# A two-layer decoder on one core: the four hand-written step orders of TensorE, VectorE, ScalarE and GpSimd rewritten

## The reference, cut to what matters

```
x = x + L0_attn(ln(x))           # m : state-space mixer: projections, a causal convolution with 16 decays, gate
x = x + L0_xattn(ln(x), ctx)     # x0: 16 heads of 8 against the context
x = x + L0_ffn(ln(x))            # s0: 16 heads of 4 over the 256 tokens, then 8 experts, the best two of each token
x = x + L1_attn(ln(x))           # s1: 16 heads of 8, 4 key heads, over the 256 tokens
x = x + L1_xattn(ln(x), ctx)     # x1: 16 heads of 8, 4 key heads, against the context
x = x + L1_ffn(ln(x))            # f : gelu(x w1 + b1) w2 + b2, 512 wide
```

## Time and profile before

| | |
|---|---|
| three runs | 727.42, 729.11, 731.83 us; median 729.11 |
| the profiled execution | span 728.7 us from first to last instruction |
| busy in that span | TensorE 634.2, VectorE 550.5, ScalarE 438.1, GpSimd 178.4 us |
| DMA | 15 GB/s mean, 10.62 MB in all |

### The profile page before, as it was taken

One profiled execution on the slowest core, in us unless ns is written; L12 is line 12 of the kernel. 1 busy time (PEld: TensorE's weight loads), 2 busy tenths in 40 slices (PEclk: granted clock), 3 DMA queues, 4 the chain that ended last, 5 costly groups with the idle time before them and its releaser, 6 DMA issues.

```text
span 728.7 us, 14858 instructions
## 1 busy us (share of the span) xinstructions
PE 634.2 (87%) x5800; PEld 430.9 (59%) x5800; DVE 550.5 (76%) x1513; ACT 438.1 (60%) x863; POOL 178.4 (24%) x348
## 2 busy tenths in 40 slices
...
DMA packets 10358, 10.62 MB, mean 15 GB/s; under 512 B 2832, under 2 KB 9520, under 8 KB 10032
## 3 DMA queue, kind: packets, MB, share of 16 engines
...
q10 hardware_dynamic: 720, 2.69, 0.9%
...
HBM read 8.60 MB, written 1.07 MB: 13 GB/s over the span
## 4 chain that ended last, share of the span: by engine, by line
PE 49%; DVE 32%; ACT 11%; issue 4%; POOL 2%; DMA 1%; ACTq 1%; SPq 0%; POOLq 0%; DVEq 0%
DVE qs L1150 8%; PE psA L1562 8%; PE psB L1549 8%; PE psO L1500 6%; ACT P L839 5%; PE psB L1476 4%; PE psA L1460 4%; PE psM L1439 4%; DVE QT L1138 4%; DVE qs L1145 3%; PE psM L1358 3%; PE psM L1315 2%; ACT QT L836 2%; DVE stats L948 1%; DVE kz_s L1131 1%
## 5 line engine op out<-in xcount | busy, mean ns | idle before, releaser
L839 ACT ACTIVATE P<-psB 128x512 f32<-128x512 f32 x320 | 176.9, 597 | 71.5 <-PE psB L1476 46.1
L1150 DVE TENSOR_REDUCE qs<-psA 128x2 bf16<-128x512 f32 x256 | 165.4, 690 | 26.6 <-PE psA L1460 25.4
L1460 PE MATMUL psA<-kz_s,QT 128*128 128x512 bf16 x256 | 90.7, 385 | 13.7 <-DVE qs L1150 8.0
L1476 PE MATMUL psB<-QT,kz_s 128*128 128x256 bf16 x512 | 90.6, 276 | 9.7 <-ACT QT L836 3.2
L846 ACT ACTIVATE P<-psB,W 128x256 f32<-128x256 f32 x160 | 66.4, 473 | 39.8 <-PE psB L1549 34.8
L1439 PE MATMUL psM<-identb,qs 128*128 128x128 bf16 x896 | 72.4, 222 | 11.0 <-DVE qs L1145 2.9
L1439 PEld LDWEIGHTS psM<-identb,qs 128*128 128x128 bf16 x896 | 56.3, 99 | 31.6 <-issue 8.0
L1500 PE MATMUL psO<-P,vp 128*32 128x256 f32 x1024 | 68.3, 385 | 2.1 <-ACT P L839 1.5
L1476 PEld LDWEIGHTS psB<-QT,kz_s 128*128 128x128 bf16 x512 | 39.2, 98 | 52.2 <-ACT P L839 26.3
L1562 PE MATMUL psA<-w,P 128*128 128x128 f32 x512 | 66.1, 277 | 1.8 <-ACT P L846 0.9
L661 POOL TENSOR_SCALAR veps<-mv 128x2 f32<-128x2 f32 x40 | 10.4, 261 | 229.2 <-DVE mv L952 228.6
...
## 6 DMA issues: line engine op xcount, KB each, us to landing
...
```

The costliest lines, as they stand in the source:

```text
L839: act.activation(P[:, p, :, :].rearrange("p a s -> p (a s)"), psB[:, s.u % B_BANKS, :], ACT.Exp, scale=LAYERS[s.L]["scale"]).then_inc(b_dr ...
L1150: dve.tensor_reduce(qs[L["W"]][j][:, t * H + h:t * H + h + 2, 0], ps.rearrange("p (h c) -> p h c", h=2), AX.X, ALU.max, negate=True).then_ ...
L1460: ins = pe.matmul(ps, QT[j][:, h // L["HB"], t * 128:t * 128 + 128], kz[s.L][j][:, kv:kv + 2, :].rearrange("p h s -> p (h s)"), start=True ...
L1476: ins = pe.matmul(ps[:, i * S:i * S + S], kz[s.L][j][:, kv + i, kc * 128:kc * 128 + 128], QT[j][:, h // L["HB"], :], start=True, stop=True)
```

## The change

Only the four strings are other; no step, instruction, buffer or semaphore is added or taken away. Counted from the strings, TensorE's has 1304 letters: 689 of them stand in 170 stretches that are written in another order, and at least 265 steps move against the rest, 215 of them by four places or fewer. VectorE: 249 of 736 letters in 71 stretches; ScalarE: 131 of 664 in 47; GpSimd: 66 of 120 in 16. Of 416 uses of a `psM` bank 50 fall in the other bank.

```diff
 ORDER = {
     "PE": (
-        "00w001010010w101000a10a1a021aawaaa1011010101b0wbb2bb0bb0000b001a001001a001aa10a0ax0aaa00aa10aa1aa1ba1a211aa1a1"
...
+        "0w0001010010w110000a10aa1021aaaawa10110101b010wbb2bb00b0b00b001a001001a100a1a00aax0aaa1a0a00aa1aab1a1a21a1aa11"
...
     "DVE": (
-        "0120w10200010w001000a11001a1w1011100b0w110b0000000100011001000x100011111111211110111x0020221aaaa22aaaa01102000"
...
+        "100w012200010w010000a11001a1w1011100b101w0b000000010001100100x1000011111211111110111x0020212a2aa2aaaaa01102000"
...
     "POOL": (
-        "021w00110w0100111x22200020021102x03111333y11224333y222444232354443333534465z664456545566z447677755776675757667"
-        "7755665677"
+        "012w0011w0001111x202200000221100x311233111232y4333224y442223354443333354465z66445555646644z7777557776665757667"
+        "7755566677"
```

More of the change, by code:

```diff
@@ L160 @@
[L160 to L164, removed]
@@ new lines @@
+        "aacaa1ccaaaca1a2a20121b01101010b2b211b112b0bbb0c0101a200a1a1aa1b1aa1111a11120b1011bb10b1b1xb1bb102bb220bb02xb2"
+        "b0bb222bb2bbcb22bcc2231cc31c2c1c2c31c21cc3cc1cc31ccc11ccb1cbb123b2b2b23b2b3y2c12223122cc122cc231ccc1233213d122"
+        "32d2dc22d2d22dd22ydc23c22c3c232c32ccc23c2c4ycc33ccd33cc433cc3c3cc333c3d32d3d3d2d432d2d33d2d3d4dd4dd2dd2yddd22d"
+        "dc2dcc234c3c3c3c434c3d332342334423dd433d2dddd23e3244e2e33e33de33ee33333de33dd34d3d34ddd43d34d34dddddd4d4dd44d5"
+        "4d4e44d44454434e3e4e4e3e443ee3ee4eee5ee3ee333eeedee3d3dedd4dd44d4454e4344354344ee434eeeee343453444e444z4566454"
@@ new lines @@
+        "46464e464e5e655e6e454ee4efe4e64fee55fzee6eefeeef6e6e6fe6f64fg444g5g45g5g5g54fg4445eg445ee655e6556e56e565e55e55"
+        "f5f5ff4f65f5fzfff455g6ff46f6fff66ff6f64ff666f64g6646gz545g65gg655ggf5757557667f7557f7f755ff7f7577ghfh7h75ghhg5"
+        "hhghf75757g5577g55hgg555g757ggg7g777g577g7776h776hh75hh765hh6h77hhf6h65g766676gh6g66g65gffgghhghh565ffhhh65hhf"
+        "ffhff566ff676ff67f6f766fff76ff667f7hg77766776h776h7hh6g5hhhgg567657gg56gg5ggg77gh77g777g7g7g7g7hgg7h5h7g7hh77g"
+        "ghh7h7h7hghh65h5h5h6hfhhh65hh65ffhff76ff7777f566656g66g5gg7g77gg7hg7hh76hh6hh56h57576766577767"
@@ new lines @@
+        "11b11233b223y3123ccc111cc3ccc23323d2122322222d2224y2322232324322y333333333333323334223323242y222c22344c334432d"
+        "444222ddddd4dd3e344333233e3333335333433434334544444444444434444334434335333d33d444435e33e3eeeeee44543444464z65"
+        "444565444465465546544f46465z56f66664g644545g545454445e454655556e655556556554655z556464666466666666z546657575f7"
+        "66f777ff77ff7f777hf775h5575577557555577755777777776777575676756g77ggg5gggg556656656676666677667h666h6hhh65hhh7"
+        "65576757767777777757777777756555f6556f76776765666g76567g777h5776h56676777567"
@@ L177 @@
     ),
     "ACT": (
[L179 to L182, removed]
```

25 lines of the change are left out of this document (10 added, 15 removed).

## The result

| | before | after |
|---|---|---|
| median of six runs each | 729.19 us (727.42 to 732.96) | 724.98 us (722.82 to 727.33) |
| ratio of the two, 95% interval | | 0.9924 (0.9902 to 0.9946) |
| span of the profiled execution | 728.7 us | 723.0 us |

Predicted were 724.6 us in a range of 715 to 734. The medians differ by 4.2 us (0.6%); the ratio's interval, 3.9 to 7.1 us, holds the forecast's 4.5.

A forecast was written before the change was run, and what follows sets the result against it. The prediction took TensorE's instruction list plus its waits to bound the kernel; gains and losses at the walked places summed to -4.5 us, taking 729.1 to 724.6 us, range 715 to 734.

The forecast's parts named there:

- The start: T3.b0 ahead of T1.b1's norm on VectorE: -0.5 us; T5.b1 ahead of Q.x0.b0.0 delays the first scores: +0.9.
- 294 and 316: TensorE waits at 294.78 and 316.48 us, filled by P4.s0.b3 (-0.75) and T5.b4 (-0.7).
- 533's +0.45: At 533.64 us H.s0.b5.0's wait for the gelu grows as two score steps leave the place ahead of it: +0.45 us.
- 162 and 230: TensorE waits at 162.46 us (F2.s1.b0, filled by R2.s0.b1: -0.4) and 230.30 us (T5.b3, behind five steps: -0.45).
- 486: At 486.84 us A.x1.b4.0's wait of 1.04 us is filled by P4.s0.b5: -0.45 us.
- 388: At 388.31 us M.s0.b4.0's wait of 0.73 us is filled by two score steps: -0.4 us.
- the five small ones: TensorE waits from K.s1.b3 (356.48 us) to V.s1.b6.0 (651.93 us), one or two score steps ahead of each: -1.5 us together.
- given back: TensorE reaches the next point sooner but waits there for VectorE: 727.7 us, chance 0.27.
- Nothing in the gelu stretches, nothing in the tail: Shuffles inside G and H stretches, and reordered VectorE work in the last 39 us, were each counted as 0.
- slower: Waiting steps written ahead of ready work; some eleven places losing 0.9 us each decide, fifteen give 736.8 us; chance 0.16.
- ScalarE counts: Exponentials pace the stretch around 600 us, so two saved table loads come off the time: 722.0 us, chance 0.08.
- The clock: Stretches at TensorE's lower clock fall elsewhere: two fewer give 720.8 us, two more 728.4; chance 0.07.

The follow-up runs named there:

- the second time: The changed kernel measured again, unaltered, beside the kernel before: 725.65 us, ratio 0.9917.
- first: The kernel before with the new order on all four engines only as far as 212 us: 729.89 us, ratio 0.9996.
- tables: The kernel before with S.s1.b5.0 moved behind the gelus on ScalarE and behind H.s0.b6.4 on TensorE, saving two table loads: 731.56 us, ratio 1.0012.
- The seven moves alone: The kernel before with only the seven walked places in new order, without their neighbours' moves: 733.48 us, ratio 1.0023.
- middle: The kernel before with the new order only from 212 to 340 us: 729.84 us, ratio 0.9986.
- gelu6: The kernel before with the new order of TensorE, VectorE and ScalarE only from 585 to 631 us: 727.81 us, ratio 0.9964.
- last: The kernel before with the new order only from 340 us on: 730.21 us, ratio 0.9999.

## Why the prediction was right, and where its steps were not

The number was right (724.6 for 724.98, and 725.65 the second time), and the sum of the stretches, -4.6, is close to the -4.5. But it came out of terms that were right for the whole order and wrong for the moves to which they were given, and of omissions that cancel, so that it came so close is in good part luck.

*The start.* -0.5 and +0.9 were counted. Measured against T1.b0's first matmul, T5.b0 ended 0.96 earlier (profiles of first and tables), and the place of T5.b1 and Q.x0.b0.0 cost 0.42: sign and mechanism right, the gain twice the forecast and the loss half of it. The gain was larger because T1.b1's norm took 1.10 us, not the 2.3 that the prediction carried over from the kernel before. By A.s0.b0.0 at 74 us 0.1 is left of both.

*Waits filled.* For the places, the terms of 294 and 316 held in their sum (-1.45 against -1.7; 282 to 299 us gave -0.4 and 299 to 322 gave -1.3), and so did 446 (-0.7 against -0.2 to -0.6); 533's +0.45 came as +0.8 and was back by 562. 162 and 230 were too small (-0.85 against -2.1, of which 0.75 is returned by 282), 486 too (with F1.x1.b4 -0.75 against -1.2), and 388 gave nothing. Four of the five small ones came to -0.8 against -1.2, because V.s1.b6.0's stretch lost 0.35. The step that failed is the reason given: "a place gains only where other, ready work is now written ahead of the waiting step" is necessary and not enough. The seven moves alone, -3.85 by the prediction, were 0.2 to 3.1 us slower. The walk did not ask which wait the moved step had filled where it stood: at 316 and 162 it had filled the very next one. The gain needed the moves around the place that were not walked through: at 316 two or three further fills for the same chain of exponentials. The rival "given back" named this, but for VectorE and at the wrong distance: at 316 what a single fill wins is gone within 1 to 2 us, at the next wait for ScalarE, while what a whole stretch wins is kept as far as it could be followed (middle from 353 to 430 us; gelu6 to 687, less 0.2).

*Nothing in the gelu stretches, nothing in the tail.* Both failed. The stretch from 585 to 631 gave -1.9 and the tail -2.1, while the gelu stretches of batches 0, 3 and 4 cost 1.4, 0.7 and 0.8, that of batch 5 0.8 which is back by 562, and 687 to 700 cost 2.3, the clock's part included. That TensorE hardly waits in such a stretch does not make its order free; and the 0.27 us were read from 600 to 620 alone, while from 585 to 631 TensorE was idle for 1.8 of 46.38 us. It was not the table loads by themselves that did it from 585 to 631; which of the other moves did was not isolated. In the tail the sentence "the same VectorE work lies between" overlooked that VectorE itself waits there for GpSimd and that work can go into that wait.

*The rival "slower".* Its mechanism is real in this change: P3.x1.b6 ahead of S.x1.b5.3 on ScalarE is of the kind, and so was the seam of last. Putting back the losing stretches brought 3.8 us, from three of the five. It needed about eleven places of 0.9 us to decide and had some five us in four places.

*GpSimd's moves at nothing* was wrong in one place, where VectorE's L1090 lost 0.54 us at 680; what of that reached the time is not separated.

*ScalarE counts* fell as a gain of its own (tables). *The clock* was given 0.07 and did matter, in both directions, as the last section says.
